# A key lookup whose first and last chunk get an order of their own: products placed in the score banks, gathers picked first, a third row buffer, the gate ahead

## What is computed

```python
query = einsum('bsh,dh->bsd', x, q_proj_w);  rq = einsum('bsd,rd->bsr', query, router_w)
rk = einsum('nd,rd->nr', aux_keys, router_w)
scores = einsum('bsr,nr->bsn', rq, rk) / sqrt(48) + reliability_mask      # 1024 keys
top_scores, top_idx = top_k(scores, 8)
learned = gelu(x @ unc_w1.T + b) @ unc_w2.T
uncertainty = clip(0.5 * log1p(var(x)) / mean(log1p(var)) + 2.5 * sigmoid(learned), 0, 5)
gate = sigmoid(gate_w1 * uncertainty + gate_bias)
out = x + gate * (softmax(top_scores) @ aux_values[top_idx])
```

## Time and profile before

| what | value |
|---|---|
| runs | 3446.32 us median of 3 (3430.61 to 3448.28) |
| the profiled execution's own time | 3430.15 us |
| its span (first to last instruction) | 3428.4 us |
| granted TensorE clock, mean | 0.965 of full |
| busy share: PE, DVE, ACT, POOL | 91%, 79%, 66%, 34% |
| the lookup | from 3143.8 us to the end of the span |

### The profile page before, as it was taken

The page is one execution under the profiler, slowest core; times in us unless marked ns, Lnnn a source line. Parts: engine busy times, 40 slices in busy tenths (PEclk is TensorE's granted clock), DMA queues, the critical chain, the costliest instruction groups (busy, mean ns, idle before and its releaser), DMA issues. The chain is left out here.

```text
span 3428.4 us, 66538 instructions
## 1 busy us (share of the span) xinstructions
PE 3114.6 (91%) x23910; PEld 1642.0 (48%) x23910; DVE 2723.4 (79%) x4060; ACT 2246.8 (66%) x4082; POOL 1153.0 (34%) x1074
## 2 busy tenths in 40 slices
PE   8958888888799998998879999999999999998885
PEld 3327777777566665776423333333333333333553
DVE  6759999999576675454888888888888888882787
ACT  5659999999300001222338888888888888886565
POOL 8749999999100000000410000000000000001785
PEclk9979999999899999999979999999999999998998
DMA  4755433320211155351420000010100010000333
GB/s 141 219 179 146 120 106 108 99 75 14 93 56 58 35 107 131 68 133 37 118 70 16 23 15 23 16 23 16 24 16 23 16 23 15 15 22 16 99 112 109
DMA packets 225146, 234.35 MB, mean 68 GB/s; under 512 B 66034, under 2 KB 167410, under 8 KB 224052
## 3 DMA queue, kind: packets, MB, share of 16 engines
q1 hardware_dynamic: 218692, 213.41, 22.7%
q0 software_dynamic: 6144, 16.79, 1.7%
HBM read 162.77 MB, written 67.37 MB: 67 GB/s over the span
## 5 line engine op out<-in xcount | busy, mean ns | idle before, releaser
L2036 DVE TENSOR_REDUCE attn_part_max<-attn_pM 128x1 f32<-128x1024 f32 x1024 | 1206.9, 1220 | 143.0 <-PE attn_pM L2092 136.3
L2016 ACT ACTIVATE attn_probs<-attn_pE 128x512 f32<-128x512 f32 x2048 | 1096.7, 600 | 151.5 <-PE attn_pE L2142 137.6
L2142 PE MATMUL attn_pE<-attn_q,attn_k_exp 128*32 128x512 bf16 x8192 | 659.1, 384 | 12.6 <-ACT attn_probs L2016 3.3
L2112 PE MATMUL attn_pA<-attn_probs,attn_v 128*32 128x512 f32 x4096 | 548.9, 595 | 0.0
L694 DVE TENSOR_TENSOR_SCAN scan_h<-scan_abar,scan_states,scan_dbu 128x512 f32<-128x512 f32 x384 | 458.9, 1285 | 0.5 <-ACT scan_abar L659 0.5
L2142 PEld LDWEIGHTS attn_pE<-attn_q,attn_k_exp 128*32 128x32 bf16 x8192 | 197.1, 95 | 514.4 <-ACT attn_probs L2016 334.3
L2091 PE MATMUL attn_pM<-attn_k_exp,attn_q 64*128 64x512 bf16 x1024 | 360.4, 393 | 43.9 <-DVE attn_part_max L2036 24.6
L708 PE MATMUL scan_hT<-scan_ident,scan_h 128*128 128x128 f32 x2048 | 322.5, 281 | 71.3 <-ACT scan_hcT L650 29.5
L650 ACT ACTIVATE scan_hcT<-scan_hT,scan_c_t 128x512 f32<-128x512 f32 x512 | 373.7, 730 | 2.0 <-PE scan_hT L708 1.8
L2092 PE MATMUL attn_pM<-attn_k_max,attn_q 64*128 64x512 bf16 x1024 | 360.4, 393 | 0.0
L1219 PE MATMUL moe_pP<-moe_w_qkv,moe_xT 128*128 128x384 f32 x1024 | 340.4, 490 | 0.9
(11 more groups left out here) (293 smaller groups left out, 3973.7 us busy)
## 6 DMA issues: line engine op xcount, KB each, us to landing
scan_b_even<-mid_BC SPq DMA_DIRECT2D x16, 1024.0 KB, 9.7
scan_b_odd<-mid_BC SPq DMA_DIRECT2D x16, 1024.0 KB, 9.5
causal_rwB<-mid_rwT SPq DMA_DIRECT2D x64, 256.0 KB, 4.6
attn_q<-mid_q_parts SPq DMA_DIRECT2D x224, 64.0 KB, 2.4
mid_gT<-front_gT SPq DMA_DIRECT2D x8, 1024.0 KB, 8.7
mid_uT<-front_uT SPq DMA_DIRECT2D x8, 1024.0 KB, 10.4
mid_dT<-scan_g_odd SPq DMA_DIRECT2D x8, 1024.0 KB, 4.3
moe_yT<-mid_yT SPq DMA_DIRECT2D x7, 1024.0 KB, 6.7
```

What stands on the lines that cost most here:

```text
L2016: nc.scalar.activation(probs[:, kt % 4, h, :], pE[:, bank(item), :], ACT.Exp, scale=SCALE).then_inc(exp_done, 1)
L2036: nc.vector.reduce_max(part_max[:, h, j, i:i + 1], pM[:, m % 2, :], AXIS_X).then_inc(max_read, 1)
L2112: last = nc.tensor.matmul(pA[32 * h:32 * h + 32, :], v[:, par, kt, :], probs[:, kt % 4, h, :], start=(kt == 0), stop=(kt == KT - 1))
L2142: last = nc.tensor.matmul(pE[32 * i:32 * i + 32, bank(item), :], k_exp[:, par, kt * 128 + 32 * i:kt * 128 + 32 * i + 32], q[:, qc, h, :], ...
```

## The change

- Start, PE: the weight products go into the scores' banks `pS` (they no longer wait for the first sum to leave `pX`); `flip_ctx(1)` moves ahead of them and of `flip_xh(0)`; `widen(0)` moves ahead of the first scores.
- Start, ACT: it takes over the three copies of the weight products from DVE, and runs two one-column activations (`warm`) that bring the Gelu's and then the exponential's table load forward.
- Last chunk, DVE: `place_top(7,1)` before `pick(7,0)`; the gate's input before both remaining picks; `place_top(7,3)` reads the score that PE now makes third and comes before `pick(7,2)`; `results` of the early chunks are spread between.
- Last chunk, PE: the one-column product for the mean and `scores(7,3)` come ahead of `lookup(6,2)`, and `scores(7,2)` behind it.
- The last gather goes into a third row buffer and waits for no sum of rows. A new wait: DVE holds `place_top(7,3)` until the rows of (6,3) have landed, since the gathers read the same `place` buffer.
- Last chunk, ACT: the gate's second sigmoid stands directly behind the first. For chunks 5 and 6 ACT multiplies by the gate (`gate_rows`) and POOL adds (two 128x1024 additions behind its last gather); DVE makes the results of the other six. SP stores in the order of chunks, and so waits for POOL's two additions before it stores chunk 7.

The diff, cut to its core:

```diff
-        rows = s.sb("rows", [128, 2, TOP, D])
+        FINAL = 2
+        rows = s.sb("rows", [128, 3, TOP, D])
...
                 for c in range(NCH):
-                    sp.wait_ge(out_ready, (c + 1) * TPC)
+                    if c in (NCH - 3, NCH - 2):
+                        sp.wait_ge(pool_out, c - (NCH - 4))
+                    else:
+                        sp.wait_ge(out_ready, (c + 1 if c < NCH - 3 else NCH - 2) * TPC)
...
+                    final = o == 2 * NCH - 1
                     if first == 0:
                         pool.wait_ge(place_ready, o + 1)
-                        at_least(pool, rows_summed, o - 1)
+                        if not final:
+                            at_least(pool, rows_summed, o - 1)
...
+                for n, c in enumerate((NCH - 3, NCH - 2)):
+                    pool.wait_ge(rows_gated, (n + 1) * TPC)
+                    pool.wait_ge(sum_kept, c + 1)
+                    pool.wait_ge(out_done[c % 4], 16)
+                    nc.gpsimd.tensor_tensor(result[:, c % 4, :, :], look_all[:, c * TPC:(c + 1) * TPC, :], sum_all[:, c * TPC:(c + 1) * TPC, :], ALU.add).then_inc(pool_out, 1)
```

VectorE's last chunk:

```diff
                 variances(ch)
+                place_top(last, 1)
                 pick(last, 0, marks + ch.n)
                 ch.n += TILE_MARKS
                 learned(last)
-                place_top(last, 1)
+                gate_input(ch)
+                dve.wait_ge(rows_in[1], last * 16 * TOP)
+                place_top(last, 3, order=2)
                 weigh(last, 0)
                 weigh_rows(last, 1)
+                weigh_rows(last, 3, FINAL)
+                dve.wait_ge(gate_ready, 1)
+                results(0)
+                pick(last, 2, marks + ch.n, order=3)
+                ch.n += TILE_MARKS
+                results(1)
+                weigh(last, 2)
                 sum_rows(last - 1, 3)
-                gate_input(ch)
-                pick(last, 2, marks + ch.n)
-                ch.n += TILE_MARKS
-                place_top(last, 3)
-                weigh(last, 2)
-                weigh_rows(last, 3)
-                dve.wait_ge(gate_ready, 1)
-                for c in range(NCH // 2):
-                    results(c)
+                results(2)
+                results(3)
                 sum_rows(last, 1)
-                for c in range(NCH // 2, NCH - 1):
-                    results(c)
-                sum_rows(last, 3)
-                results(last)
+                results(4)
+                sum_rows(last, 3, FINAL)
+                results(last, (0, 1, 3))
+                results(last, (2,))
```

ScalarE's start and its last chunk:

```diff
+                act.wait_ge(x3_psum, 2)
+                move_ctx(1)
+                act.wait_ge(qr_psum, 1)
+                nc.scalar.activation(w_qr[:], pS[:, 1, 0:D].rearrange("p (k n) -> p k n", k=KD), ACT.Copy).then_inc(qr_ready, 1)
+                for i in range(2):
+                    act.wait_ge(rk_psum, i + 1)
+                    nc.scalar.activation(rk[HIGH * i:HIGH * i + RD, :], pS[HIGH * i:HIGH * i + RD, 0, i * CH:(i + 1) * CH], ACT.Copy).then_inc(rk_moved, 1)
+                act.wait_ge(one_set, 1)
+                act.wait_ge(rest_in, 16 * REST_LOADS)
+                nc.scalar.activation(warm[:], rq_one[:], ACT.Gelu).then_inc(warmed, 1)
                 move_xh(0)
...
                 hidden(0)
+                act.wait_ge(warmed, 1)
+                nc.scalar.activation(warm[:], rq_one[:], ACT.Exp).then_inc(warmed, 1)
...
+                act.wait_ge(unc_ready, 2)
+                nc.scalar.activation(gate[:], gate[:], ACT.Sigmoid, bias=scalars[:, 2:3], scale=scalars[:, 1:2]).then_inc(gate_ready, 1)
                 expo(last, 0)
                 expo_rows(last, 1)
+                expo_rows(last, 3)
                 scale_rows(last - 1, 3)
                 finish(last - 1, 2)
                 move_weights(2 * last)
...
                 expo(last, 2)
-                expo_rows(last, 3)
+                act.wait_ge(gate_ready, 1)
+                gate_rows(last - 2)
                 scale_rows(last, 1)
                 finish(last, 0)
                 move_weights(2 * last + 1)
+                scale_rows(last, 3, FINAL)
+                gate_rows(last - 1)
                 finish(last, 2)
-                scale_rows(last, 3)
```

TensorE's last chunk (`ahead` is 0 there):

```diff
                     if ahead:
                         x3_pair(c + 1, 1)
-                    scores(c, 2, cpar)
+                        scores(c, 2, cpar)
+                    else:
+                        pe.wait_ge(const_set, 2)
+                        pe.wait_ge(lsum_ready, 1)
+                        nc.tensor.matmul(pX[:, 0:1], ones[:], tmp_v[:, 0:1], start=True, stop=True).then_inc(lsum_psum, 1)
+                        scores(c, 3, cpar)
                     if not first:
                         lookup(c - 1, 2)
+                    if not ahead:
+                        scores(c, 2, cpar)
```

More of the change, by code:

```diff
@@ L2402, in results @@
                         dve.wait_ge(out_done[c % 4], 16)
-                    for j in range(TPC):
+                    for j in tiles:
                         n = c * TPC + j
@@ L2679, in _ @@
                 scores(0, 1, 0)
-                pe.wait_ge(rest_in, 16 * REST_LOADS)
-                widen(0)
                 learn(0)
@@ L2702, in body @@
                         project(c + 1)
-                    else:
-                        pe.wait_ge(const_set, 2)
-                        pe.wait_ge(lsum_ready, 1)
-                        nc.tensor.matmul(pX[:, 0:1], ones[:], tmp_v[:, 0:1], start=True, stop=True).then_inc(lsum_psum, 1)
-                        scores(c, 3, cpar)
                     if ahead == 2:
```

64 lines of the change are left out of this document (32 added, 32 removed).

## The result

| | before | changed |
|---|---|---|
| median of 20 runs each | 3440.19 us (3429.27 to 3448.28) | 3428.31 us (3421.07 to 3433.75) |
| ratio | | 0.9969, 95% interval 0.9960 to 0.9978 |
| the profiled execution's own time | 3430.15 us | 3433.51 us |
| its span | 3428.4 us | 3431.4 us |
| granted TensorE clock, mean | 0.965 | 0.964 |

The account below looks back on a forecast made before the run. The prediction took the last chunk to be a POOL gather queue with a tail, and the start a PE chain. Its terms summed to -7.5 us, from 3446.3 to a median of 3438.8, likeliest 3439, range 3418 to 3447.

Parts of the forecast that it names:

- The tail: Last chunk, first gather of (7,1) to the span's end: POOL's wait, gathers, landing and work behind it, forecast -8.2 us.
- (b): Last chunk, POOL's wait for VectorE's places before the gathers of (7,3): 5.08 becomes 0.30, -4.8 us.
- (c): Last chunk, length of POOL's gathers: (7,1) 11.85 for 13.35, -1.5 us; (7,3) 13.5 for 15.73, -2.2 us.
- (d): Last chunk, landing of the last gather: 6.0 before, falls to the median 4.0, -2.0 us.
- (a): Last chunk, gathers of (7,1) start earlier because `place_top(7,1)` comes ahead of `pick(7,0)`: -0.3 us.
- (e): Behind the last landing, scaling, gate, POOL's addition, VectorE's results and stores run serially: 14.9 for 12.6, +2.3 us.
- The start: Lookup's start: PE idles 6.3 us for chunk 1's loads, partly paid back later; `root(1)` comes later, +1.0 us.
- the lower level: Lookup's start, PE clock at 1.2 GHz behind the gap: first scores +6.2 us, `root(1)` +1.5.
- the higher level: Lookup's start, PE clock at 2.4 GHz behind the gap: first scores +3.0 us, `root(1)` -1.6.
- The gathers run undisturbed: Rival: last chunk's gathers undisturbed and the start at the higher level, -17.0 us, median 3429.3; chance 0.17.
- The gain doesn't come: Rival: POOL's wait goes, but gathers of (7,3) starve under VectorE's run as before, -0.1 us; chance 0.15.
- Slower, the clock: Rival: low PE clock lasts through the next sum, start costs 10.5, whole +2.0 us; decides above 8.5; chance 0.06.

Follow-up runs that it names:

- x8: Changed kernel without the third row buffer, so the last gather again waits for the sum of the rows of (6,3): 3436.77 us, ratio 0.9996 to the kernel before.
- x5: The changed kernel run again, nothing altered, on the second chip: 3431.73 us, ratio 0.9984 to the kernel before.
- x10: The changed kernel run a third time, nothing altered, on the third chip: 3420.26 us, ratio 0.9974 to the kernel before.
- x12: Changed kernel with one added wait: VectorE stands still after the weights of (7,3) until its rows have landed; one run, 3430.62 us.
- x6: Changed kernel with all results of chunks 0 to 4 moved behind the last sum of rows of (7,1): 3431.85 us, ratio 0.9982 to the kernel before.
- x1: Kernel before with only the changed start: 3427.43 us, ratio 1.0000 to the kernel before.
- x9: The kernel before run once more, unchanged, on the third chip: 3426.65 us, ratio 0.9992.
- x4: The kernel before run once more, unchanged, on the first chip: 3427.40 us, ratio 0.9999.
- x7: Changed kernel with chunk 1's context transposes (`flip_ctx(1)`) and their copies put back behind the projection: 3426.09 us, ratio 0.9968 to the kernel before.
- x2: Changed kernel with the start of the kernel before, so the changed end alone: 3420.23 us, ratio 0.9975 to the kernel before.
- x3: Changed kernel with ScalarE's `gate_rows(6)` and `finish(7,2)` moved ahead of the last scaling: 3418.49 us, ratio 0.9973 to the kernel before.
- x11: Changed kernel with chunk 6's gate and `finish(7,2)` ahead of the last scaling, and `flip_ctx(1)` behind the projection: 3417.13 us, ratio 0.9962 to the kernel before.

## Why the prediction was right, and where it was not

**The tail, -7.0 for a forecast of -8.2 by the same cuts.** The terms:

- (b), POOL's wait, 5.08 to 0.30: as forecast, and for the reason given. The last places come 6.2 behind those of (7,1), as the prediction counted. x8 shows what the third buffer, which the prediction named in one sentence as the other thing that POOL could wait for, is worth: without it the wait is 7.05, longer than the 5.08 of before. That the buffer alone would give nothing either follows from the earlier trace rows, where VectorE's places ended the wait; it was not run.
- (c), the gathers: (7,1) -1.26 for -1.5, (7,3) -2.51 for -2.2 (-3.4 in x5, -4.0 in x10). Mechanism and size held, and x12 with x6 shows the mechanism. The prediction said "now and then for a whole run of them", and the run of 12 results that held the last gather of before to 2.86 is gone: that gather takes 1.21 in the first profile of the changed kernel. One bound was wrong: (7,1) cannot come down to 9.7, since a pause of 1.94 stands behind its first gather. It is 2.05 before, 2.43 in x12, and 1.86 or more in every profile but x1's, where it is 0.64 and POOL had stood 3.20 ahead of that gather. It is not a long gather, and the prediction's bound counted it as one. The profile calls it issue; its cause stays open.
- (d), the landing, forecast -2.0: this is the term that was off, by counting twice. The 6.00 of the earlier trace rows hold the last gather's own 2.86, which is also in the 15.73 that (c) shortens. From that gather's end to the scaling it took 3.22 before (3.23 in x9, 2.60 in x4) and takes 3.15 in the first profile of the changed kernel, 1.97 in x5 and 1.99 in x10: against the first profile of before, the landing by itself gained 0.1 to 1.2. The rest of the -2.0 is the gather's own, told twice. The lesson of the two views is that a chain's DMA entry starts at the issuing instruction's start.
- (a), the earlier start of (7,1), -0.3, did not come: POOL stands 0.76 ahead of that gather (0.77 in x10), and stood 0.63 before. In the lengths it would be too small for the middle's scatter: x10's middle is 0.2 shorter than that of before and 0.7 shorter than x9's.
- (e), behind the landing, +1.61 for +2.3: as forecast in kind. VectorE's third addition starts 0.34 into POOL's and ends 0.27 behind its end, results from 3425.11. The Trainium skill (SBUF — State Buffer, Who interferes with whom) says that the two exclude each other; 2.44 for 0.42 agrees. The same section's inference that such a VectorE instruction does not hold up the making of a gather's descriptors does not hold here: long gathers end 0.82 behind it, and among the last eight of x12, which have no such instruction beside them, there are none.

These sum to -1.26 - 4.77 - 2.58 + 1.61 = -7.0, with (c) and (d) taken together as 18.95 to 16.37. How far the long gathers fall on the last eight differs between executions of one kernel: the changed kernel's tails are 42.9, 40.9 and 40.2, those of before 49.9, 50.5 and 49.6. By their means the tail gives 8.7. Two sums of the prediction are slightly off: (e)'s 14.9 adds up to 14.8, and the bounds at their good end to -18.8, not -19.3.

**The start, -0.1 for a forecast of +1.0.** The gap is there and longer than said (6.51 for 6.3), and the clock is at the lower level behind it. But it rose while the key products ran, which took 2.56 in place of the 3.8 forecast, so the case lies nearer the higher level. And `root(1)` does not wait for the sum alone: its list has three gathers ahead of it, from 3181.16 to 3184.88, which the prediction did not count; its variance is ready at 3184.13. x1 shows it in the times. The prediction's sign for this step was right in one way: x7 shows 4.5 us of `root(1)` that the moved transposes give away, paid back by the rest of the new start.

**The rivals.** "The gathers run undisturbed" is out for the changed kernel (two or three long ones in each profile) and true in x12 for (7,3) alone. "The gain doesn't come" is out: POOL's wait went and the gathers of (7,3) did not starve again, and 15 of the 20 runs of before are slower than the slowest of the changed kernel. "Slower, the clock": its bound of 8.5 at the start was not reached. ScalarE, named as what would make it wrong, was in time: it stood 8.65 before the last rows.

**The size in the times.** The prediction put the median at 3438.8, and it is 3428.31, 10.5 lower. Of these, 6.1 are its base, the median of three runs at 3446.32, where twenty gave 3440.19; the other 4.4 are the gain, 11.9 between the medians for 7.5. The three comparisons of the changed kernel give ratios of 0.9969, 0.9984 and 0.9974, or 10.7, 5.5 and 8.9 us; their intervals (7.6 to 13.8, 2.4 to 8.6, 5.1 to 13.0) share 7.6 to 8.6. Tail and start of the profiles sum to 7.1, or 8.8 by the means, and x2, without the new start, gave 8.6. The forecast of -7.5 (without (a), -7.2) stands so near to 7.1 by two errors that cancel: the tail 1.2 too good, through the landing, and the start 1.1 too dear.

**The middle that was 10 us longer.** The first profile of the changed kernel and x5, x6, x7 and x8 have a middle of 199.8 to 203.6, all others 189.8 to 195.2. Timeline of the first one's VectorE and TensorE in chunk 4, with the second half of the next sum and the next transposes:

```profile
3301.61 0.76 DVE L2316 TENSOR_TENSOR look_x<-look_pX,look_x 128x256 f32<-128x256 f32 x2 [3.99 <-DMA rot_w_qk<-in_w_qk]
```
```profile
3308.67 1.94 PE L2622 MATMUL look_pT<-look_ident,look_xh 128*128 128x128 f32 x8 [5.41 <-DVE look_xh L2341]
```

The same transposes in x10, the same code:

```profile
3299.58 1.06 PE L2622 MATMUL look_pT<-look_ident,look_xh 128*128 128x128 f32 x8 [1.49 <-DVE look_xh L2341]
```

And the eight microseconds from the transposes on, x10 and the first profile:

```profile
3299.00:3307.00 8.00, 6.19 (x36) 4.80 (x37) 7.68 (x17) 4.37 (x8) 6.76 (x7) 1.00 0.29 87
```
```profile
3308.00:3316.00 8.00, 6.10 (x20) 4.38 (x21) 7.68 (x17) 2.17 (x4) 6.76 (x7) 0.52 0.28 82
```

VectorE stands 3.99 ahead of the second addition, where x10 shows no idle time, TensorE stands 5.41 ahead of the transposes where it stood 1.49, and they run at half the clock (1.94 for 1.06); their granted clock is 0.52 where x10 has 1.00. Theory B of x9 and x10, that the changed code does it by itself, is out: x10 has 192.8, and the kernel before has one such place of its own in x9, a smaller one:

```profile
3326.89 1.94 PE L2592 MATMUL look_pT<-look_ident,look_xh 128*128 128x128 f32 x8 [2.30 <-DVE look_xh L2329]
```

What makes the addition late is open, and that the changed code has a part in it is not excluded: all five long middles are of kernels with changed code. x5 to x8 ran on one chip, on which the kernel before was never profiled. Two things suggest that it suffers too. Its median there, 3437.79, is 8.7 above the higher of the other two, about the size of the longer middle. And its 20 runs of the first comparison lie in two groups, 5 from 3429.27 to 3432.42 and 15 from 3437.20 to 3448.28. No profile shows it.

## What to carry to other kernels

Where a queue of gathers ends a kernel, look at both things that a gather waits for, its indices and its buffer, before moving either: here the early places without the third buffer gave 1.0 of 6.1 us. Look also at what runs beside the gathers: here a run of 12 results without a gap held one to 2.86, and in the changed kernel, with results in fours and eights, no gather of the last eight takes over 2.42. Work that is moved onto an idle engine near the end belongs ahead of the last arrival (x3) if it is itself ready by then (in x11 it was not), and here an addition of POOL's beside VectorE's last one cost 2 us. When terms are read from a chain of waits and from a timeline, cut the time at the same points for both, or one duration is counted in two terms.

## What the hardware showed that was not expected

- Each of the 218 gathers of over 1.3 us ends 0.81 to 0.85 behind a VectorE instruction with two inputs in SBUF, nearly always one over 128x1024 numbers. Beside results of 128x256 a gather can take 0.95 or 1.21, or be held through several, to 2.86 (before, x1, x4, x9); in x4 one beside eight results and then an addition of rows took 4.79. What decides between these is not shown. With VectorE still, eight took 0.94 to 0.95 each.
- POOL's 128x1024 addition makes a VectorE addition of 0.42 take 2.44, and four results of 1.67 take 6.72 beside two of them.
- When the granted clock comes back differs between executions of nearly one code: projection and the transposes behind it took 3.75 and 1.91 in x11, 3.34 and 1.04 in x7. From the start of the one to the end of the other it is 5.45 and 4.21, which is 1.24 of the 1.36 between their `root(1)` (38.44 and 37.08).
- Three chips ran the kernel before at 3429.0, 3429.1 and 3437.8: they differ by as much as the change is worth, so only runs on one chip compare.
